# One-core Mamba block and mixture of experts: the side work of sixteen scan steps at other places, raw weight pieces fetched ahead of C's rows

## The reference

```
x_and_res = x @ W_in.T;  xp, res = split(x_and_res)
xc  = silu(causal_conv(xp, 4 taps) + conv_b)
ssm = xc @ W_x.T          # B (16), C (16), dt (1) of each token
dt  = softplus(dt @ W_dt.T + b_dt)
h   = exp(A * dt) * h + dt * B * xc      # a scan over the tokens, for each of 16 states n
y   = sum_n h[n] * C[n] + D * xc
x   = layernorm(x + silu(y + res) @ W_out.T)
top-2 of softmax(x @ router.T);  x = layernorm(x + sum_k weight_k * expert_k(x))
```

## Time and profile before

| | us |
|---|---|
| median of 3 runs (lowest, highest) | 1413.18 (1409.65, 1415.11) |
| profiled execution, whole | 1412.16 |
| its span in the profile | 1410.5 |
| start of block 0's first scan | 40.2 |
| block 0, block 1 | 104.5, 101.0 |
| blocks 2, 3, 4, 5 | 100.6, 101.8, 100.6, 101.5 |
| block 6, block 7 | 96.4, 95.5 |
| from the last scan to the end of the span | 568 |

### The profile page before, as it was taken

The page is one execution under the profiler, slowest core; times in us unless marked ns, Lnnn a source line. Parts: engine busy times, 40 slices in busy tenths (PEclk is TensorE's granted clock), DMA queues, the critical chain, the costliest instruction groups (busy, mean ns, idle before and its releaser), DMA issues. The chain is left out here.

```text
span 1410.5 us, 28835 instructions
## 1 busy us (share of the span) xinstructions
PE 1278.5 (91%) x8807; PEld 1086.4 (77%) x8808; DVE 1100.4 (78%) x1836; ACT 992.8 (70%) x1364; POOL 1052.1 (75%) x920
## 2 busy tenths in 40 slices
PE   5799899999999999999997995599999999999990
PEld 2478687788787787887886884599999999999980
DVE  6879989889899899899898895666656665666554
ACT  6899998998999999999988863343344334433434
POOL 3489798798999989999989997455555555555445
PEclk9799999999999999999999997799999999999995
DMA  8523132132232332332322337425555723522216
GB/s 279 179 78 100 49 121 79 57 119 78 77 124 83 103 101 69 109 105 76 106 76 78 122 96 259 126 43 116 121 154 149 206 40 79 137 40 39 34 20 246
DMA packets 91017, 150.75 MB, mean 107 GB/s; under 512 B 10892, under 2 KB 43276, under 8 KB 90928
## 3 DMA queue, kind: packets, MB, share of 16 engines
q1 hardware_dynamic: 73216, 121.24, 26.2%
q0 software_dynamic: 16704, 27.29, 9.8%
q10 hardware_dynamic: 1008, 1.07, 0.3%
HBM read 100.79 MB, written 48.78 MB: 106 GB/s over the span
## 5 line engine op out<-in xcount | busy, mean ns | idle before, releaser
L1445 POOL TENSOR_TENSOR arena<-arena 128x1024 f32<-128x1024 f32 x252 | 599.0, 2391 | 10.3 <-DVE arena L1107 4.2
L492 PE MATMUL d_ps<-ident,arena 128*128 128x128 f32 x2048 | 318.8, 279 | 35.3 <-DVE arena L1107 29.0
L492 PEld LDWEIGHTS d_ps<-ident,arena 128*128 128x128 f32 x2048 | 242.6, 143 | 135.5 <-issue 60.6
L1107 DVE TENSOR_TENSOR_SCAN arena<-arena,carry,d_ps 128x512 f32<-128x512 f32 x256 | 314.5, 1265 | 27.5 <-PE d_ps L492 20.4
L793 ACT ACTIVATE arena<-u_tok,b_tok 128x512 f32<-128x512 f32 x508 | 324.4, 711 | 6.3 <-PE d_ps L492 5.1
L1107 DVE TENSOR_TENSOR_SCAN arena<-arena,d_ps 128x512 f32<-128x512 f32 x256 | 301.2, 1207 | 31.4 <-PE d_ps L492 21.0
L505 PE MATMUL y_ps<-ident,arena 128*128 128x128 f32 x2048 | 297.4, 274 | 7.0 <-POOL arena L1445 5.5
L1794 ACT ACTIVATE h_t<-ht_ps 128x512 f32<-128x512 f32 x142 | 84.5, 595 | 284.1 <-PE ht_ps L1849 284.1
L807 ACT ACTIVATE arena<-dt,neg_a 128x2048 f32<-128x2048 f32 x127 | 253.1, 1993 | 1.4 <-DVE arena L1107 1.4
L505 PEld LDWEIGHTS y_ps<-ident,arena 128*128 128x128 f32 x2048 | 237.3, 142 | 11.5 <-POOL arena L1445 7.7
L1834 PE MATMUL h_ps<-arena,xg_t 128*128 x852 | 217.5, 404 | 1.3 <-DVE xg_t L1926 1.3
(11 more groups left out here) (230 smaller groups left out, 1541.9 us busy)
## 6 DMA issues: line engine op xcount, KB each, us to landing
arena<-c_rows SPq DMA_DIRECT2D x128, 256.0 KB
arena<-weight_parts SPq DMA_DIRECT2D x20, 1024.0 KB, 5.3
weight_parts<-arena SPq DMA_DIRECT2D x64, 256.0 KB
xg<-expert_rows POOLq DMA_DIRECT2D x71, 130.0 KB
arena<-in_pieces SPq DMA_DIRECT2D x16, 512.0 KB, 9.3
arena<-in_pieces SPq DMA_DIRECT2D x64, 128.0 KB, 3.3
expert_out<-arena SPq DMA_DIRECT2D x1, 4224.0 KB, 15.2
weight_parts<-arena SPq DMA_DIRECT2D x4, 1024.0 KB, 4.6
```

Source lines behind the costliest of these rows:

```text
L492: last = nc.tensor.matmul(d_ps[:, c % 2, j * P:(j + 1) * P], ub[:, g % U_RING, j, c * P:(c + 1) * P], t.ident[:], start=True, stop=True, i ...
L1107: nc.vector.tensor_tensor_scan(h[:, g % H_RING, c, :], decay[:, g % D_RING, c, :], d_ps[:, c % 2, :], 0.0 if i % 2 == 0 else carry[:, n, c ...
L1445: nc.gpsimd.tensor_tensor(h[:, g % H_RING, lo:hi, :], h[:, g % H_RING, lo:hi, :], c_row[:, g % C_RING:g % C_RING + 1, :].broadcast_to([P, ...
```

## The change

It moves side work to other places and changes nothing that is computed. The number of operations of each kind is the same. On ACT, `z_part` now stands at four places, `silu` ahead of step 2's `scale` (behind `turned_out(0)`), `yt_copy` at the end of step 2, `size_log` ahead of step 7's `decays`, `router_exp` in step 5, `normed` ahead of step 13's `scale`, and `xp_out` at the end of steps 11 and 14 and the start of 13. On POOL, `rstds` now stands ahead of step 11's first product, `router_den` and `router_member` ahead of theirs, and the eight `send_rows` at steps 14, 15, 15, 0, 0, 2, 4, 4 where they stood at 13, 13, 13, 15, 1, 1, 1, 2. On SP, `fetch` stands ahead of `load_c`. The bank of `logits` is 1 where it was 0. The diff, cut to its core (`...` marks what is left out):

```diff
-        PIECE_STEPS = (1, 3, 4, 6, 7, 9, 10, 12)
+        PIECE_STEPS = (2, 3, 5, 6, 7, 9, 10, 12)
...
-                    if 0 <= g + LEAD < STEPS:
-                        load_c(g + LEAD)
                     piece = piece_of(*divmod(g - 2, STATE))
                     if piece is not None:
                         fetch(piece + PARTS_RING)
+                    if 0 <= g + LEAD < STEPS:
+                        load_c(g + LEAD)
...
-        GATE_AT = ((5, 0), (5, 1), (5, 2), (5, 2), (6, 0), (8, 3), (9, 1), (9, 3))
-        IN_AT = (((11, 2), (11, 2)), ((12, 0), (12, 1)), ((15, 0), (15, 0)), ((15, 2), (15, 3)))
+        GATE_AT = ((5, 1), (5, 1), (5, 1), (5, 2), (6, 1), (8, 3), (8, 3), (9, 1))
+        IN_AT = (((11, 1), (11, 1)), ((12, 1), (12, 1)), ((15, 0), (15, 0)), ((15, 2), (15, 3)))
...
-        TAP_AT = (((12, 0), (12, 1), (12, 3)), ((13, 3), (14, 2), (14, 3)), ((15, 0), (15, 1), (16, 2)),
-                  ((16, 3), (17, 0), (17, 1)))
+        TAP_AT = (((12, 0), (12, 1), (12, 2)), ((14, 0), (14, 2), (14, 3)), ((15, 1), (15, 2), (16, 2)),
+                  ((16, 3), (17, 1), (17, 2)))
...
-                        if at == (0, 3):
+                        if at == (1, 3):
                             turn(0)
-                        if at == (4, 1):
+                        if at == (3, 0):
                             turn(1)
...
-                            if at == (10, 1):
+                            if at == (9, 3):
                                 inputs(0)
-                            if at == (11, 2):
+                            if at == (10, 3):
                                 inputs(1)
...
-                            if at == (5, 0):
+                            if at == (4, 3):
                                 router_pick()
...
-                            if at == (13, 2):
+                            if at == (15, 1):
                                 router_place()
```

## The result

The changed kernel takes 1423.23 us (median of 5 runs, 1421.66 to 1426.86) against 1415.11 (5 runs, 1409.65 to 1416.81): 1.0065 times as long, 95% interval 1.0051 to 1.0079. That is about 9 us slower, 1 us above the end of the range on record (1402 to 1422), and above the 1420.2 from which the prediction speaks of slower and to which it gave 0.22.

The account below looks back on a forecast made before the run. Block length was taken as PE's time from (2, 2) to the next (0, 0), plus DVE's to (2, 2). Blocks +2.4, seam -2.2, about 0 together, and small waits -1.5 gave 1410.7 profiled, 1411.5 forecast; range 1402 to 1422.

Parts of the forecast that it names:

- The sends on POOL: Later `send_rows`: one indirect DMA of 1.27 us less before block 6's last product; elsewhere POOL has slack of 1 to 3.
- the seam: Between blocks 6 and 7, where PE waits 3.01 and 1.27 us for POOL: 2.2 us less was forecast.
- rival D: Slower because POOL becomes the bound, through late products, sums at (1, 3) and `y_silu`: 1420 us, chance 0.07.
- `inputs`: Moved to (9, 3) and (10, 3) on DVE, waiting for POOL products: costs 0.85 us per even block, 1.45 per odd.
- forecast A: Gains and port waits cancel out, `inputs` taking near 2.0 us: 1411.5 us, from 1407 to 1418, chance 0.51.
- the cover of 0.25: Slack before PE's fourth `sizes_again` at (10, 0) in an even block, to absorb part of the `inputs(0)` wait: 0.25 us.
- The bounds: Limits on what one `inputs` pays for starting within a POOL product: 0 and 1.9 us, mean 1.1.
- Steps 0 to 4: PE's wait at (4, 1) for `yt_copy` falls from 0.46 to 0.1: 0.65 us less per even block, 0.3 per odd.
- Step 13: Earlier tap ends PE's wait before `turn_u(0)`: 0.49 us less per even block, 0.4 per odd; `turn_u(2)` waits 0.35.
- SP: `fetch` ahead of `load_c`: C's row goes out later but is wanted over 9 us on; worth nothing.
- Small waits: Unpriced waits, such as `add_sizes(0)` for ACT at step 8 and raw pieces, rather go than come: 1.5 us off.
- ACT's `scale` or `decays` late at steps 9 or 13: Named sign that the forecast is wrong; no row of the profile before showed either as late.

Follow-up runs that it names:

- b_rstds: The kernel before with only POOL's `rstds` moved ahead of step 11's first product: 1412.62 us, ratio 0.9988.
- a_sends: The changed kernel with the eight `send_rows`, `halo_fix`, `router_spread` and `router_place` back at their old places: 1418.57 us, ratio 1.0030.
- a_pool: The changed kernel with all of POOL's order, and `router_sum`, `router_invert` and `router_place` on DVE, put back: 1464.03 us, ratio 1.0354.
- the swap: On DVE, `add_sizes(2)` ahead of `inputs(0)`: 1.0065 to 1.0045 on the changed kernel, 1.0030 to 1.0002 on that kernel with the sends put back.
- s_swap: The changed kernel with the sends and what they need put back, and `add_sizes(2)` ahead of `inputs(0)` on DVE: 1414.76 us, ratio 1.0002.
- b_tap: The kernel before with the third tap of the first quarter at (12, 2), not (12, 3): 1413.64 us, ratio 1.0000.
- b_fetch: The kernel before with `fetch` ahead of `load_c` on SP: 1414.46 us, ratio 1.0002.
- a_fetch: The changed kernel with `load_c` ahead of `fetch` on SP again: 1440.94 us, ratio 1.0182.
- a_one: The changed kernel with `inputs` reading one SBUF tile, multiplied by a constant, without the product with `dt`: 1416.51 us, ratio 1.0019.

## Why the prediction was wrong

**The sends on POOL: the step that failed.** I priced them only where they helped, at the seam, and wrote that elsewhere POOL has a slack of 1 to 3 us. The seam came near what I had priced (4.3 to 2.75, where I had written "down to about 2"; block 7 1.3 shorter), but by luck: I had counted 1.9 for `rstds`, and with `rstds` at its new place and the sends at the old ones PE's waits there are 4.4 (b_rstds) and 4.6 (a_sends). But the slack of 0.8 and 2.28 in even blocks is all POOL has, in blocks 3 and 5 there is none, and two DMAs more in steps 0 to 6 (2.6 us) with the wait of 2.69 use it up. What hung on it I named only in part: `router_exp`, which stands earlier on ACT, the raw pieces, and `normed` ahead of `scale`. `halo_fix` at step 0 I didn't price at all. Measured by a_sends: 0.35%, 5 us. The change of blocks 2 to 6 against before says the same. On record were +0.06 for an even block and +0.75 for an odd one; measured are +0.1, -0.4, +1.1, +1.8, +6.1, and with the sends back +0.2, +0.7, +0.2, +0.6, -0.1. It is rival D, given 0.07 for 1420: in block 5 by the sums of step 1, as written there (PE's 1.50 for POOL), in blocks 4 and 6 by `router_exp` and `ut_out`, which it didn't name.

**`inputs`: mechanism right, size short.** The durations are near 2.0, as forecast A said (mean 1.92, with starts anywhere in a product), and the wait is PE's for the fourth `sizes_again`, as written. I took 0.55 to 0.65 for it; PE stood 0.68 in block 2 and 1.28 in block 4, where `add_sizes(0)` had already waited 0.92 for `size_log`, which is likely what used up the cover of 0.25 that I counted (no run isolates it). I also left out block 0, where PE stood 2.10 (1.07 before), and priced block 1, where it stood 1.27, as a steady one. The bounds had an error too: an `inputs` that starts with the product and ends 1.1 after it pays 2.3 and not 1.9 (a_pool has one of 3402 ns); the mean of 1.1 stands. Measured by the swap: 0.2 to 0.3%, 3 to 4 us, most of it in blocks 0 and 1.

**What the two parts explain.** With both undone, s_swap takes what the kernel before takes (interval 0.9988 to 1.0015). By blocks that is a balance and not the old state: blocks 2 to 7 still take 3.2 us more than before, 1.7 of it in block 7 (6.8 us at the 1.2 GHz level and not 3.4) and 0.6 in each of blocks 3 and 5, and blocks 0 and 1 take 3.9 less, of which 1.6 also differs in equal code. Which moves leave the 0.6 in an odd block wasn't tested.

**Steps 0 to 4.** The wait at (4, 1) is 0.13 in block 4 (0.1 forecast), but 0.38 in block 5, where I had expected none.

**Step 13.** No wait stands ahead of the first `turn_u` any more, and the third waits 0.37 in block 4, for which I had 0.35. b_tap shows that this gain was never there to take: in even blocks the next wait, for ACT, was as long, in odd ones DVE's road held. I had looked for what is late next and found ACT covered.

**SP.** Worth nothing by itself, as recorded (b_fetch). What was wrong is to price it against the old POOL: with POOL late it is worth 17 us, since the old order would cost that much there (a_fetch).

**Small waits.** The 1.5 us that I let go without a price did not go.

Of what would have made me wrong, I named "ACT's `scale` or `decays` late at steps 9 or 13": in block 6 it is `scale` at step 13.

What stays open: why the first scan comes up to 2.6 us earlier or later in equal code, and what decides the 60.9 to 63.8 us from the end of the last scan to the experts' first `h_t` (61.0 before, 62.4 in the changed kernel, 61.2 in a_one, 63.8 in b_rstds).

## What to carry to other kernels

In an order written out by hand on several full engines, add up the slack of each engine between two points where it waits, and charge every moved instruction to it, also of the engine that isn't the bound: here 3 us of POOL's slack in every second block decided. Ask of each moved consumer (`router_exp`) whether its producer is still early in the new order, and price a queue's order (`fetch`) with the lateness that the rest of the change makes. An edit that is free alone can cost in company and the other way round, so undo by groups that hang together, and look at the first blocks apart from the steady ones.

## What the hardware showed that I had not expected

A `tensor_scalar` on DVE with one SBUF tile (693 ns alone) waits for a running POOL product just as a product of two tiles does (2.33 us, ending 0.55 us after the product); the scans, which read one SBUF tile and one in PSUM, keep 1.2 us beside the same products. It works both ways: two products in a row, 4.71 us where neither became due while `inputs` ran, take 5.69 where `inputs` runs as the second becomes due, and 5.17 beside the shorter form. And two stops of PE of 1.99 and 0.80 us close together cost more than their length, since 5.2 us at the 1.2 GHz level followed; in the kernel before, the single stop of 3.01 at the seam was followed by 3.4 us at it.
